# Chunk 1 of a long convolution: spectra of even and odd rows combined on VectorE instead of by TensorE's negated constants

## The reference

```
xz = einsum('bld,ed->bel', hidden, W_in);  x, z = split(xz, 2)
x  = silu(conv4(x) + conv_b)
y  = irfft(rfft(x, 2L) * rfft(k_ssm, 2L))[..., :L]      # k_ssm has 512 taps
y  = (y + x * D_skip) * silu(z)
out = einsum('bhl,dh->bld', y, W_out)
x  = layernorm(hidden + out)
```

## Time and profile before

| | us |
|---|---|
| median of 3 executions | 454.08 (452.54 to 455.95) |
| profiled execution, device time | 453.8 |
| its span, first to last instruction | 452.0 |
| busy PE / DVE / ACT / POOL | 409.1 / 337.3 / 192.9 / 21.8 |
| mean granted clock of TensorE, share of full speed | 0.964 |

### The profile page before, as it was taken

One profiled execution on the slowest core, in us unless ns is written; L12 is line 12 of the kernel. 1 busy time (PEld: TensorE's weight loads), 2 busy tenths in 40 slices (PEclk: granted clock), 3 DMA queues, 4 the chain that ended last, 5 costly groups with the idle time before them and its releaser, 6 DMA issues.

```text
span 452.0 us, 4385 instructions
## 1 busy us (share of the span) xinstructions
PE 409.1 (91%) x1494; PEld 215.4 (48%) x1494; DVE 337.3 (75%) x688; ACT 192.9 (43%) x318; POOL 21.8 (5%) x38
## 2 busy tenths in 40 slices
PE   4791987979999999999999889999999999999992
PEld 1341565667976375354544343433644433443361
DVE  5999998977882996879988994697654862374565
ACT  1342669452226513445255355344055626225431
POOL 1000203021000000000000000000000000000001
PEclk9896999879999999999999989999999999999997
DMA  6300000040000000000000000000000000000001
GB/s 227 133 1 0 1 1 0 2 151 0 1 1 0 1 1 0 0 1 1 1 1 0 0 1 23 0 1 1 0 0 1 24 1 0 1 0 0 0 1 46
DMA packets 4886, 7.10 MB, mean 16 GB/s; under 512 B 1031, under 2 KB 3713, under 8 KB 4737
## 3 DMA queue, kind: packets, MB, share of 16 engines
q1 hardware_dynamic: 3932, 4.78, 3.1%
q10 hardware_dynamic: 933, 2.04, 1.3%
HBM read 5.78 MB, written 1.05 MB: 15 GB/s over the span
## 4 chain that ended last, share of the span: by engine, by line
PE 64%; DVE 13%; ACT 3%; issue 2%; POOL 1%; POOLq 0%; DVEq 0%
PE ring L1291 21%; PE ring L1271 6%; PE ring L1286 4%; PE bankA L198 4%; PE ring L1273 3%; PE ring L1299 3%; PE ring L1306 2%; PE ring L1313 2%; PE ring L1310 2%; PE ring L1317 2%; PE timebank L300 2%; PE bankA L300 2%; PE specbank L275 2%; PE ring L1308 2%; PE ring L1314 1%
## 5 line engine op out<-in xcount | busy, mean ns | idle before, releaser
L1291 PE MATMUL ring<-hm,wc 128*128 128x512 f32 (+1 forms) x252 | 108.6, 581 | 0.0
L1291 PEld LDWEIGHTS ring<-hm,wc 128*128 128x128 f32 x252 | 46.2, 190 | 61.0 <-issue 53.0
L1500 DVE SCALAR_TENSOR_TENSOR hm<-xtm,cst,h 128x512 f32<-128x512 bf16 x48 | 33.2, 746 | 2.7 <-ACT h L1405 2.7
L198 PE MATMUL bankA<-wconv,h2w 128*128 128x256 f32 x128 | 35.0, 425 | 0.0
L1419 ACT ACTIVATE gts<-ring 128x512 f32<-128x512 f32 (+1 forms) x18 | 9.9, 550 | 49.0 <-PE ring L1291 49.0
L1405 ACT ACTIVATE h<-ring,vec 128x512 f32<-128x512 f32 x32 | 21.9, 686 | 17.7 <-PE ring L1273 15.2
L198 PEld LDWEIGHTS bankA<-wconv,h2w 128*128 128x128 f32 x128 | 26.0, 212 | 5.5 <-issue 2.0
L1589 DVE SCALAR_TENSOR_TENSOR f2e<-hl,f2e 128x512 f32<-128x512 f32 (+1 forms) x9 | 5.7, 631 | 26.1 <-ACT hl L1450 26.1
L1286 PE MATMUL ring<-hm,wc 64*128 64x512 f32 (+1 forms) x84 | 22.9, 621 | 1.2 <-DVE hm L1500 1.2
L1271 PE MATMUL ring<-zs,wc 128*128 128x512 f32 x40 | 20.9, 603 | 0.3 <-DVE zs L1591 0.3
L1416 ACT ACT_TABLE_LOAD x8 | 10.3, 1283 | 25.1 <-PE ring L1291 25.1
(11 more groups left out here) (274 smaller groups left out, 791.3 us busy)
## 6 DMA issues: line engine op xcount, KB each, us to landing
wc<-in_w_c SPq DMA_DIRECT2D x1, 1664.0 KB
out<-xall SPq DMA_DIRECT2D x8, 128.0 KB, 1.9
cst<-in_const ACTq DMA_DIRECT2D x1, 838.5 KB, 10.7
wc<-in_x_feat SPq DMA_DIRECT2D x1, 768.0 KB, 11.7
wc<-in_k_time ACTq DMA_DIRECT2D x1, 512.0 KB
bconv<-in_bcast SPq DMA_DIRECT2D x1, 512.0 KB, 10.7
wc<-in_x_feat ACTq DMA_DIRECT2D x1, 256.0 KB, 3.7
wa<-in_w_a SPq DMA_DIRECT2D x1, 256.0 KB, 3.8
```

The lines of the kernel that those rows point to most:

```text
L198: ins = pe.matmul(at, h2w[:, n, u % 2, u // 2:u // 2 + P], wconv[:, tap, :], start=False, stop=(h == HALVES - 1 and tap == TAPS - 1))
L1291: ins = pe.matmul(dst[:, at], wc[:, w:w + P], hm[:, seat(j, made + g - 1), at], start=False, stop=(g == PAIRS - 1))
L1500: dve.scalar_tensor_tensor(hm[:, seat(j, k), :], picked, cst[:, C_EG + g:C_EG + g + 1], h[:, g, :], ALU.is_equal, ALU.mult).then_inc(S["hm ...
```

## The change

The two tuples that name the folded and unfolded chunks get chunk 1 as a member.

```diff
-FOLDED, UNFOLDED = (2, 3), (2, 3)
+FOLDED, UNFOLDED = (1, 2, 3), (1, 2, 3)
```

## The result

The changed kernel takes 456.28 us (median of 20, 455.25 to 457.24) against 453.90 for the kernel before in the same 20 rounds: a ratio of 1.005, with an interval of 1.0036 to 1.0063. That is 2.4 us more; 1.9 had been forecast.

A forecast was written before the change was run, and what follows sets the result against it. The prediction took how late VectorE is at each hand-over to TensorE as the bound, not TensorE's busy share. A tail start 0.05 us later plus 1.85 us of clock gave +1.9 us on the median 454.08: 456.0 us, range 452.6 to 458.8.

The forecast's parts named there:

- rival A: The forecast itself: PE's saving becomes waiting and the clock falls once; 456.0 us, chance 0.50.
- What is removed and added: Chunk 1's transforms: PE saves 7.0 us in all, DVE gets 2.66 us a half, 5.3 us in all.
- Stage 1: To the first turn, 112 to 133 us: forward half's saving gone, PE waits 1.8 us; net +0.1 us.
- Stage 2: Turn to masks, 133 to 149 us: ScalarE's copy of the spread moves up; net -0.65 us.
- Stage 3: Products to tail, 149 to 172 us: xn +2.0 us, PE stands 4.3 us, tail starts +0.05 us.
- The clock: Behind PE's 4.3 us pause at the tail: one fall to half speed, priced at 1.85 us.
- Nothing is given back: Behind the tail and forward (2,0): the rest of the chain shifts as a whole and recovers nothing.
- B: No clock fall, or one ending before PE works again: +0.65 us, 454.7 us; chance 0.18.
- C: A second clock fall at the turn of chunk 0, another 1.7 us: 457.7 us; chance 0.12.
- D: DVE is the bound throughout, its whole 5.3 us land on the end: 459.4, with a fall 461; chance 0.07.
- E: PE is the bound, its 7.0 us come off: 447.1 us; chance 0.05.
- F: DVE has more slack than seen at one of two places, 1 to 4 us stay: about 451.5; chance 0.08.

The follow-up runs named there:

- fold_only: Kernel before with chunk 1 folded in the forward transform but not unfolded before the inverse; 454.09 us, ratio 1.0003.
- inverse_twice: Changed kernel with TensorE doing chunk 1's short inverse twice, signalling after the second; 454.76 us, ratio 1.001.
- changed_both_filled: Changed kernel with chunk 1's inverse done twice and three unread matmuls in the wait at 258 us; 454.45 us, ratio 1.0009.
- unfold_only: Kernel before with chunk 1 unfolded before the inverse, forward transform unchanged; 455.85 us, ratio 1.0028.
- fold_filled: fold_only with three unread matmuls put in TensorE's wait for chunk 2's choice at 258 us; 451.90 us, ratio 0.9922.

## Why the prediction was right

The forecast (456.0, range 452.6 to 458.8) and its rival A were right: PE's saving becomes waiting and the clock falls once. The steps, with the common zero of above:

- **What is removed and added.** The inverse took 3.73 us in the timeline, where the long one of fold_only takes 7.31, and L327 to L345 is 1.32 us apart in both halves (119.00 to 120.32 for the first). Both as forecast.
- **Stage 1.** The tiles were 0.64 late, as worked out. The turn was 0.35 late, not 0.1. What was left out is the hand-over: before, PE went from the pieces into this turn without a wait, the first transpose overlapping the end of the last piece; now it starts 0.15 us after DVE's end (133.85 to 134.00), and the overlap of 0.16 is lost.
- **Stage 2.** ScalarE's copy moved to 145.88, a shift of -0.45 against -0.65. ScalarE's own timeline shows it held by DVE's `gap` and its tanh, which are as late as the turn:

```profile
145.76 0.21 ACT L1381 ACTIVATE tg<-gap 128x4 f32<-128x4 f32 x1 [0.41 <-DVE gap L1486]
145.88 1.07 ACT L1384 ACTIVATE xtm<-ring 128x512 bf16<-128x512 f32 x2
```

- **Stage 3.** xn is +2.20 (forecast +2.0), the difference being the two terms above. PE's wait is 4.41 us (forecast 4.3). The tail's start is +0.53 against +0.05: again 0.2 from before, and a hand-over of 0.15 (xn ends at 170.63, L1306 starts at 170.78) in place of an overlapped start.
- **The clock.** It fell, to 0.51 for 3.4 us. The forecast priced it at 1.85 us with the wait for L387 inside. Measured: 1.5 by the medians of changed and inverse_twice, 1.1 by the shifts of the two at the tail's end (+2.23 and +1.12). The term was somewhat too large and the hand-overs too small, and the two misses made up for each other: +2.23 at the tail's end against the forecast's +1.9. That much of the agreement is luck.
- **Nothing is given back.** That held in the schedule, as changed_both_filled shows, but not for the clock: the profile of the changed kernel has no fall at 262 us where the one before had, worth 0.7 us, so its end is only 1.53 late. The forecast took the later falls as they were.

The rivals: B (no fall) and C (a second fall at the turn) did not occur. D, that DVE bounds everything, fails at stage 1, where DVE won back 1.7 us of waiting at the first gate. The rule of the Trainium skill beside it (Perfetto Trace Analysis, Identifying the Most-Contended Engine) points at VectorE and in sign it was right, but the amount was not DVE's 5.3 us. E, that PE bounds, is out by all three of changed, unfold_only and fold_only. F, that DVE has more slack, is out too: xn ended 0.2 later than forecast, not earlier. For C, the windows of the changed kernel around the turn:

```profile
131.90:134.70 2.80, 0.89 (x6) 0.69 (x6) 1.97 (x5) 0.64 (x2) 0.80 (x1) 1.00 0.00 0
134.70:141.00 6.30, 6.30 (x15) 2.33 (x14) 2.77 (x5) 5.55 (x9) 0.00 (x0) 1.00 0.00 0
```

A wait of 1.9 us and then four transposes left the clock at 1.00. The Trainium skill's sentence on transposes (TensorE: Matmul & The Clock Gate, Part 4) isn't refuted by this, but no fall followed from it here. In the first part of the kernel before, four transposes stand between waits of 1.25 and 1.40 us, and the fall at 95 us follows; no run separates the transposes from the waits.

**What the prediction did not say.** The change has two parts, and they meet different stages. Folding gives DVE its work where DVE has about the room, and pays 1.5 us; unfolding gives it the same work where PE would finish early and wait, and costs about 2. The parts don't add up one by one: with chunk 1 unfolded, xn sets the tail, and folding as well brings the tail's start forward by 0.18 us only (+0.71 to +0.53), where alone it brought 1.81. The prediction worked out both in one sum and did not say that half of the change was the better kernel.

## What to carry to other kernels

Work taken from the busiest engine is worth at most the slack of the engine that hands it its next input, read at that hand-over from start times; if an edit has parts, do the sum for each part alone. When the busiest engine is TensorE, count what a new wait does to its clock, and compare variants with the clock's falls in view: fold_only looked worthless until a wait elsewhere was filled. Waits of TensorE that lie ahead of a stretch at half clock are places for useless matmuls into a free bank, a little shorter than the wait. It pays only where TensorE is the later engine behind them: the stretch at 78 us gave nothing, the one at 95 us 0.9 us or more.

## What the runs showed of the hardware that was not expected

- Adding work to TensorE made kernels faster: 1.5 us for 3.57 us of repeated inverse (inverse_twice), 2.2 us for 2.6 us of unread matmuls (fold_filled against fold_only).
- One and the same wait of 2.9 us (L1252 at about 258 us) was followed by no fall of the clock, by one of 3.4 us or by one of 6.9 us, in profiles of kernels that differ by a few us ahead of it. The spread of the kernel before from 452.5 to 457.1 us goes with it: with this wait filled no execution took more than 454.43. Beside fold_only, its seven executions of 456.2 us and more have mean clocks of 0.959 to 0.962, the other 28 of 0.964 to 0.971.
- A stretch at half clock can be free: behind 78 us TensorE's slower work was covered by a later wait for VectorE (0.51 us with the fall, 2.19 without, L708 at the same distance).
- A matmul that is released by VectorE starts 0.05 to 0.15 us after that instruction's end (0.15 at L1226 and L1306 of the changed kernel, 0.05 to 0.06 at L1286 and L1271), and does not overlap the end of the matmul before it, which back-to-back ones do by about 0.16 us in these timelines, whose matmul ends are modelled.
